# A transformer tower on one core: score groups turned in three blocks of 384 columns, and the end of the feed-forward written out

## The reference

```
h = keep the 179 best tokens of each batch (score x @ w, top k)
h = h + attention0(layernorm(h))   # 12 heads of 16
h = h + ffn0(layernorm(h))         # 192 -> 768 -> 192, weights, gelu and output rounded to a grid
h = h + attention1(layernorm(h))   # input rounded on ONE scale for all batches
h = h + experts(layernorm(h))      # 16 experts, each token goes to the best one

attention0: score[t, s] = sum_d tanh(q[t, d] + k[s, d]) * ws[d] + bs;  softmax over s;  @ v
attention1: xq = round(x / scale) * scale, scale = max|x| / 127 over all of x
            softmax with 2^floor(z) * (1 + frac z), z = logits / ln 2 - max
```

## Time and profile before

| what | value |
|---|---|
| device time, three runs | 1414.4 us median (1407.2 to 1414.99) |
| the profiled execution, its own time | 1418.28 us |
| its span, first to last instruction | 1416.4 us |
| PE busy | 1154.0 us (81%) |
| DVE busy | 1106.0 us (78%) |
| ACT busy | 1000.7 us (71%) |
| POOL busy | 862.3 us (61%) |
| mean granted clock of TensorE | 0.938 |

### The profile page before, as it was taken

How to read it: one execution, slowest core, us unless ns; L and a number is a source line. 1 busy time by engine, 2 the same in 40 slices (tenths; PEclk the granted TensorE clock), 3 DMA queues, 4 the chain that set the end, 5 groups by cost and what they waited for, 6 DMA issues and landing times. The chain is left out here.

```text
span 1416.4 us, 39002 instructions
## 1 busy us (share of the span) xinstructions
PE 1154.0 (81%) x16164; PEld 875.3 (62%) x16164; DVE 1106.0 (78%) x2109; ACT 1000.7 (71%) x921; POOL 862.3 (61%) x978
## 2 busy tenths in 40 slices
PE   4776888788878887887888779857999999998496
PEld 3454665566556655665556458844677777776496
DVE  8789999999999999999999958862556767675343
ACT  0479999999999999999999967732244334442142
POOL 4088888888888888889888976450012222123354
PEclk9899999999999999999999999975799999998598
DMA  9999998000000000000000011000000100001352
GB/s 251 360 359 359 355 341 294 4 2 3 2 2 2 2 2 2 2 3 2 2 2 2 2 33 37 0 1 1 1 2 10 54 17 18 18 17 32 98 157 62
DMA packets 75449, 103.06 MB, mean 73 GB/s; under 512 B 6303, under 2 KB 73640, under 8 KB 75282
## 3 DMA queue, kind: packets, MB, share of 16 engines
q1 hardware_dynamic: 63784, 87.90, 18.9%
q10 hardware_dynamic: 6860, 6.12, 1.7%
q0 software_dynamic: 4640, 6.65, 1.4%
HBM read 18.32 MB, written 83.85 MB: 72 GB/s over the span
## 5 line engine op out<-in xcount | busy, mean ns | idle before, releaser
L918 ACT ACTIVATE work<-work 128x2864 f32<-128x2864 f32 (+1 forms) x272 | 695.1, 2637 | 12.3 <-DVE work L437 11.4
L437 POOL TENSOR_TENSOR work<-shared 128x1253 f32<-128x1253 f32 (+1 forms) x272 | 613.7, 2266 | 130.5 <-PE psum L1786 94.2
L1786 PE MATMUL psum<-work,ws_place 128*32 128x179 f32 x8640 | 394.2, 321 | 150.2 <-ACT work L918 148.1
L437 DVE TENSOR_TENSOR work<-psum,shared 128x1611 f32<-128x1611 f32 (+3 forms) x288 | 487.9, 1722 | 0.6
L1786 PEld LDWEIGHTS psum<-work,ws_place 128*32 128x32 f32 x8640 | 257.0, 110 | 257.7 <-ACT work L918 205.5
L1975 PE MATMUL psum<-shared 32*64 32x179 f32 (+1 forms) x1728 | 140.3, 365 | 4.4 <-DVE peaks L1481 3.8
L1975 PEld LDWEIGHTS psum<-shared 32*64 32x64 f32 (+1 forms) x1728 | 80.6, 157 | 48.6 <-issue 35.4
L907 ACT ACTIVATE pt_region<-psum,bs_neg 128x512 f32<-128x512 f32 x144 | 104.3, 725 | 2.8 <-PE psum L1799 2.8
L805 POOL DMA_INDIRECT xs_dram<-w_store,slot_i x24 | 27.0, 1126 | 110.1 <-DVE slot_i L1588 90.7
L1276 DVE SCALAR_TENSOR_TENSOR p_sb<-psum,bs_col,s_top 128x358 f32<-128x358 f32 x144 | 82.2, 570 | 15.3 <-PE psum L1799 0.6
L1799 PE MATMUL psum<-ident,p_sb 128*128 128x128 f32 x544 | 91.6, 289 | 0.0
(11 more groups left out here) (365 smaller groups left out, 2002.2 us busy)
## 6 DMA issues: line engine op xcount, KB each, us to landing
xs_dram<-pad_row SPq DMA_DIRECT2D x23, 3088.0 KB, 27.6
pt_region<-xs_dram ACTq DMA_DIRECT2D x19, 193.0 KB
pt_region<-xs_dram SPq DMA_DIRECT2D x19, 193.0 KB, 2.4
xs_dram<-pad_row SPq DMA_DIRECT2D x1, 2895.0 KB, 27.1
work<-in_x SPq DMA_DIRECT2D x2, 768.0 KB, 10.2
work<-in_x ACTq DMA_DIRECT2D x2, 768.0 KB, 16.5
work<-in_L_ffn_W2T SPq DMA_DIRECT2D x1, 1536.0 KB
work<-in_L_ffn_W1T SPq DMA_DIRECT2D x1, 1536.0 KB
```

Of the source, the lines that this page charges most:

```text
L437: ins = eng.tensor_tensor(dst[:, a * KEEP:e * KEEP].rearrange("p (u s) -> p u s", s=KEEP), k[:, h * KP:h * KP + KEEP].unsqueeze(1).to_broa ...
L918: act.activation(a, a, ACT.Tanh).then_inc(tanh_done, 1)
L1786: ins = pe.matmul(bank_s[p % 2][32 * quad:32 * quad + 32, at:at + KEEP], ws_place[:, j, :], arg_slot(n)[:, u * KEEP:(u + 1) * KEEP], start ...
```

## The change

Five edits.

1. `p_sb` has a row of 192 (`ROW`) per group in place of 179, so that a full pair fills 384 columns: 128 + 64 keys of the first group, 128 + 64 of the second. `turn_duo` makes three blocks of it in place of four: block 0 holds keys 0 to 127 of the even group, block 1 keys 128 to 191 of the even group and 0 to 63 of the odd one, block 2 keys 64 to 191 of the odd one. `exps` takes 384 columns into three planes; the last pair of one group has two blocks as before.
2. In blocks 1 and 2 the keys stand on other partitions than in `v_sb`, so each batch needs V a second time in that order, `v_extra`. Three transfers on SP's queue copy it (64, 64 and 51 partitions), each batch after `v_ready`; the 24 fills of `xs_dram` are issued four to a batch after them, for the first six batches, in place of all at the start. `context` waits for the copy (`v_spread`).
3. `context` handles even and odd groups apart: rounds 0 and 1 are 16 products each of 96 columns, round 2 is 32 of 48 columns.
4. The end of the feed-forward is written out on DVE. Statistics come ahead of `norm_max`; the hidden layer of batch 15 is rounded before the output of batch 14 is added, and its product goes to `bank_pre`, so it doesn't wait for that addition. POOL normalises batches 12 and 13 itself; DVE computes mean and 1 / deviation of batches 14 and 15 (`last_pair`), which POOL's `pair_norms` then leaves out.
5. The maximum over partitions is a transpose on PE and a reduction on DVE in place of `partition_all_reduce`. `warm_up` has 8 products in place of 12 and waits for batch 13's maximum. Q, K and V of batch 0 have four banks (`qkv_bank`), and their waits go; `score_round(0, 1)` waits for what used to be waited for earlier.

The diff, cut to its core (counters of semaphores that only shift are left out):

```
+ROW, HALF_K, LAST_K = 192, 64, KEEP - 64
-        p_sb = [sb(f"p_sb{n}", [128, KEEP + WIDE]) for n in range(2)]
+        p_sb = [sb(f"p_sb{n}", [128, 2 * ROW]) for n in range(2)]
...
+        def qkv_bank(c, fill):
+            if isinstance(c, int) and c == 0:
+                return (bank_pre, bank_out, bank_s1, bank_pta)[fill]
+            return bank_out if fill else bank_pre
...
+            for b in range(B):
+                n, v = b % 2, v_sb[b % 2]
+                sp.wait_ge(v_ready, b + 1)
+                need(sp, v_spread[n], 48 * (b // 2))
+                sp.dma_start(v_extra[n][HALF_K:128, 0, :, :], v[0:HALF_K, 0, :, :]).then_inc(v_spread[n], 16)
+                sp.dma_start(v_extra[n][0:HALF_K, 1, :, :], v[HALF_K:128, 0, :, :]).then_inc(v_spread[n], 16)
+                sp.dma_start(v_extra[n][HALF_K:LAST_K, 1, :, :], v[0:TB, 1, :, :]).then_inc(v_spread[n], 16)
+                for k in range(4 * b, min(4 * b + 4, FILLS)):
+                    fill(k)
...
-            with pool.Fori(0, B // 2) as j:
+            with pool.Fori(0, B // 2 - 1) as j:
                 pair_norms(j, 0)
-            pool.wait_ge(x_maxed, 1)
-            pool.partition_all_reduce(x_allmax[:, :], x_max[:, :], 128, RMAX).then_inc(x_alled, 1)
+            for b in (B - 4, B - 3):
+                for t, rows in TILES:
+                    k = 2 * (b % 2) + t
+                    ins = pool.tensor_scalar(xn3[0:rows, 2 * b + t, :], resid[0:rows, b + 1, t, :], tmean[0:rows, k:k + 1],
+                                             trstd[0:rows, k:k + 1], ALU.subtract, ALU.mult)
+                ins.then_inc(norm_used, 1)
...
-                act.activation(pt[b % 2][:, :, 256 * k:256 * k + 128 * w],
-                               bank_pt[p % 2].rearrange("p (s c) -> p s c", s=2)[:, :, 0:128 * w],
+                act.activation(pt[b % 2][:, 0:w + 1, k, :],
+                               bank_pt[p % 2][:, 0:128 * (w + 1)].rearrange("p (s c) -> p s c", c=128),
                                ACT.Exp, bias=bs_neg[:, :], scale=1.0).then_inc(exp_done, 1)
...
-                    dve.tensor_scalar(p_sb[n][:, 2 * KEEP:KEEP + WIDE], p_sb[n][:, 2 * KEEP:KEEP + WIDE], bs_col[:, :], None, ALU.add)
+                    dve.tensor_scalar(p_sb[n][:, :], p_sb[n][:, :], bs_col[:, :], None, ALU.add)
...
-            staged(dve, ffn_step, (2, 5))
+            staged(dve, ffn_step, (2, 5), closed=True)
+            ffn_add(B - 4)
+            hidden_round(B - 3, 1)
+            dve.wait_ge(f_added, B - 3)
+            dve.wait_ge(stats_taken, B - 4)
+            pair_tile_stats(B - 3, 0)
+            norm_max(B - 7, 1)
+            ffn_add(B - 3)
+            hidden_round(B - 2, 0)
+            dve.wait_ge(f_added, B - 2)
+            pair_tile_stats(B - 2, 1)
+            norm_max(B - 6, 0)
+            hidden_round(B - 1, 1)
+            ffn_add(B - 2)
+            last_stats(0)
+            norm_max(B - 5, 1)
+            ffn_add(B - 1)
+            last_stats(1)
+            last_pair()
+            for b in range(B - 4, B):
+                norm_max(b, b % 2)
             dve.wait_ge(x_alled, 1)
+            dve.tensor_reduce(x_allmax[:, :], bank_k0[:, 0:128], AX.X, ALU.max).then_inc(x3_step, 1)
...
-                for a in range(duo(k)):
-                    for s in range(2):
-                        ins = pe.transpose(bank[:, 256 * s + 128 * a:256 * s + 128 * a + 128],
-                                           src[:, a * KEEP + 128 * s:a * KEEP + 128 * s + 128], ident[:, :])
+                for s in range(duo(k) + 1):
+                    ins = pe.transpose(bank[:, 128 * s:128 * s + 128], src[:, 128 * s:128 * s + 128], ident[:, :])
...
+                keys = [pt[n][:, s, :, :].rearrange("p k (i c) -> p k i c", c=32) for s in range(3)]
+                parts = [[(v_sb[n][:, 0, :, :], keys[0]), (v_sb[n][:, 1, :, :], keys[1])],
+                         [(v_extra[n][:, 0, :, :], keys[1]), (v_extra[n][:, 1, :, :], keys[2])]]
                 if r < 2:
+                    spans = [(KP * r, 16 * r, ((0, 6, 0), (0, 6, 16)))]
                 else:
+                    spans = [(100 * m, 16 * m, ((6, 9, 16), (5, 8, 0))) for m in range(2)]
...
             pe.wait_ge(f_added, B)
-            warm_up(12)
+            pe.wait_ge(n3_step, B - 2)
+            warm_up(8)
+            pe.wait_ge(x_maxed, 1)
+            pe.transpose(bank_k0[:, 0:128], x_max[:, 0:1].to_broadcast([128, 128]), ident[:, :]).then_inc(x_alled, 1)
```

More of the change, by code:

```diff
@@ L303, in build @@
         v_ready = sem("v_ready")
+        v_spread = [sem(f"v_spread{n}") for n in range(2)]
         args_dve = sem("args_dve")
@@ L322, in build @@
         wf_loaded = sem("wf_loaded")
-        w_step = sem("w_step")
         w_maxed = sem("w_maxed")
@@ L452, in staged @@
                     step(body * j + par, par)
-            for i in range(last, count + behind):
+            for i in range(last, last if closed else count + behind):
                 step(i, i % body)
@@ L575, in _ @@
             pool.memset(mx3[:, :], 0.0).then_inc(w1_step, 1)
+            for n in range(2):
+                pool.memset(v_extra[n][:, :, :, :], 0.0)
             pool.memset(pad_row[:, :], 0.0).then_inc(pad_ready, 1)
@@ L725, in _ @@
             pool.wait_ge(wq_step, 6)
-            pool.memset(stage[2][:, 1, 0:D], 0.0)
+            for n in (2, 3):
+                pool.memset(stage[n][:, 1, 0:D], 0.0)
             pool.memset(ew2[:, 1, :], 0.0).then_inc(ew_blank, 1)
@@ L1417, in norm_max @@
             def norm_max(b, par):
-                dve.wait_ge(pair_norm, b - par + 2)
+                last = isinstance(b, int) and b >= B - 2
+                means, rstds, first = (mean, rstd, 2) if last else (tmean, trstd, 0)
+                if isinstance(b, int) and B - 4 <= b < B - 2:
+                    dve.wait_ge(norm_used, b + 3)
+                    top_abs(b)
+                    return
+                if not last:
+                    dve.wait_ge(pair_norm, b - par + 2)
                 if isinstance(b, int) and b == 0:
@@ new lines, in last_pair @@
+            def last_pair():
+                cols = slice(2, 6)
+                mE, mO, vE, vO = (stats[:, cols, c] for c in (1, 4, 2, 5))
+                m, d, v, h, g, y, s = (a[:, cols] for a in (mean, diff, var, std, newt, rstd, above))
+                dve.tensor_tensor(m, mE, mO, ALU.add)
+                dve.tensor_tensor(d, mE, mO, ALU.subtract)
+                rlink(dve.tensor_tensor(v, vE, vO, ALU.add))
+                dve.tensor_scalar(m, m, 0.5, None, ALU.mult)
+                dve.tensor_scalar(v, v, 1.0 / D, EPS, ALU.mult, ALU.add)
+                rlink(dve.scalar_tensor_tensor(d, d, 0.25, d, ALU.mult, ALU.mult))
+                rlink(dve.tensor_tensor(v, v, d, ALU.add))
+                dve.tensor_scalar(h, v, -0.5, None, ALU.mult)
+                rlink(dve.tensor_copy(g, v.bitcast(I32)))
+                rlink(dve.tensor_scalar(g, g, -0.5, 1597463007.0, ALU.mult, ALU.add))
+                rlink(dve.tensor_copy(y.bitcast(I32), g))
+                for n in range(3):
+                    rlink(dve.tensor_tensor(s, y, y, ALU.mult))
+                    rlink(dve.tensor_tensor(s, s, h, ALU.mult))
+                    rlink(dve.scalar_tensor_tensor(y, s, 1.5, y, ALU.add, ALU.mult))
@@ L1806, in context @@
                 if r < 2:
-                    spans = [(0, UA // 4, 16 * r, col)]
+                    spans = [(KP * r, 16 * r, ((0, 6, 0), (0, 6, 16)))]
                 else:
-                    spans = [(UA // 4, PT_COLS // 32, 16 * n, col + UB * n) for n in range(2)]
-                for lo, hi, c, at in spans:
-                    for s, tile in ((0, first), (1, second)):
+                    spans = [(100 * m, 16 * m, ((6, 9, 16), (5, 8, 0))) for m in range(2)]
+                for at, c, groups in spans:
+                    for odd, (lo, hi, shift) in enumerate(groups):
@@ L1816, in context @@
+                            for step, (v, key) in enumerate(parts[odd]):
+                                ins = pe.matmul(cols, v[:, 4 * r + j, :], key[:, lo:hi, :, c + 4 * j:c + 4 * j + 4],
+                                                start=(step == 0), stop=(step == 1))
                 return ins
@@ L1952, in qk_mm @@
                     need(pe, ctx1_ready, c - 1)
-                if fill == 2:
+                if fill == 2 and c:
                     pe.wait_ge(qk_out, ROUNDS * c + 2)
                 x = xqT[c % 2]
-                bank = bank_out if fill else bank_pre
+                bank = qkv_bank(c, fill)
                 for col in range(2):
```

147 lines of the change are left out of this document (85 added, 62 removed).

## The result

| | before | after |
|---|---|---|
| median of 12 runs each | 1413.97 us | 1402.76 us |
| profiled execution | 1418.28 us | 1402.21 us |
| its span, mean granted clock | 1416.4 us, 0.938 | 1400.0 us, 0.942 |

A forecast was written before the change was run, and what follows sets the result against it. ACT, without idle time, bounds the first attention; a single-file chain at half clock bounds 930 to 998 us. Terms -12.8 + 0.6 + 0.3 - 3.8 - 2.4 - 2.7 - 1.5 = -22.3 us from median 1414.4 gave 1392, range 1380 to 1406.

The forecast's parts named there:

- The exponentials (-12.8): First attention: 128 exponentials go from 512 to 384 columns, 0.100 us each, -12.8 us, as nothing covers ACT.
- the one on `context` and the fills: First attention: doubled `context` products fit in PE's idle time, fills and V copies land in time: nothing for each.
- Rival B: First attention: DVE becomes the bound and all 12.8 us are lost, 1405; chance 0.13.
- Rival C: First attention: short `context` products cost over 25 ns each, POOL is late, ACT waits, 1440; chance 0.05.
- The end of the feed-forward (-3.8): Feed-forward end: the new order has POOL's chain as the later one, maximum at 951.6 instead of 955.38, -3.8 us.
- The maximum (-2.4): After the feed-forward: the maximum over partitions moves from POOL to PE, 4.26 us down to 1.8, -2.4 us.
- Q, K and V (-2.7): Batch 0, second attention: 40 products run without waits and the clock rises some 5.2 us in, 8.54 to 5.8, -2.7 us.
- the clock (-1.5): Second attention's first scores run at full clock for two to three rounds, -1.5 us; rest of batch 0 at half clock.
- part 2: Feed-forward end through batch 0's first scores: terms of 3.8, 2.4, 2.7 and 1.5, together 10.4 us.
- Rival A: Second attention: the clock stays up for all of batch 0, 6 to 8 us more gain, 1385; chance 0.17.
- D: Batch 0: clock does not rise in the dense run, -2.1 instead of -2.7, nothing for scores, 1394; 0.65 including the forecast.
- The start (+0.3): Kernel start: DVE adds the bias to 384 columns of two buffers in place of 77, +0.3 us.

The follow-up runs named there:

- e12: e6 repeated in more rounds: 1384.53 us, ratio 0.9786.
- e7: The changed kernel, fills in place, with the context's second round moved from group 5 to group 6: 1407.54 us, ratio 0.9965.
- e3: The kernel before with only the new feed-forward end, the maximum by TensorE and four banks for batch 0's products: ratio 0.9924.
- e9: e6 with the maximum over partitions taken by GpSimd again: 1389.22 us, timed once.
- e10: e6 with batch 0's Q, K and V products in two banks again: 1401.98 us, timed once.
- e5: The kernel before with its 23 fills moved as in e1: ratio 1.0015.
- e1: The changed kernel with fills moved: four at batch 0, then two a batch behind the context rounds: 1391.14 us, ratio 0.9877.
- e6: The changed kernel with four fills a batch, those of batches 1 to 5 behind the context rounds: 1387.56 us, ratio 0.9816.

## Why the prediction was wrong

**The exponentials (-12.8): right as a term, wrong in the sum.** 0.11 us each, and 12.4 to 13.5 us off the stage in each of the seven kernels in which fills and doubled context don't meet (732.93 to 734.04 against 746.44). As built the stage gave 2.2. Of the 11.3 us between after and e12 9.7 are ACT's waits; 1.4 are ACT's own busy time in the stage (733.09 and 731.71 us), for which no cause is shown.

**The failed step** is the one on `context` and the fills, costed apart and each at nothing. In its place the runs show PE without instructions where the two meet, ACT 9.7 us without sums, and all but 2.2 of the 12.8 us lost. The rule I set, that ACT waits only if PE is late by over 3 us in one place, was right in kind and too mild: the stalls of the four pairs, 2.5 to 4.6 us each in sum, cost ACT 1.1 to 4.6. I bounded the delay by the records' own duration (0.5 and 0.8 us), and that bound held: 64 records of 96 columns take 475.05 to 476.40, 1.35 us where I had allowed 1.7. I gave the fills "nothing" for their bytes. What I did not ask is what else uses the DMA engines while they are full: PE's own instructions. The page of the kernel before had the row of q8 (127 packets, 2.08 MB), and the GB/s slices showed full engines to 250 us; the two together, with the number of records that the change puts in one place, should have raised the question, though no row of before has the 7 us that a block takes. Rival B, whose time I gave as 1405, came nearest in number and is wrong in cause: DVE is at 95% and loses nothing from 500 us on. Rival C had the right shape (PE late, POOL late, ACT waits) and the wrong cause and size.

**The end of the feed-forward (-3.8).** 130.79 to 125.92, -4.9. Two other kernels with the old end have 128.93 and 129.08, so it is worth 3 to 5 us. (e7, which has the new end, has 129.89; its cause is open.) The +0.6 for the longer `context` at the head of this stage did not come: it is 125.92 with it and 125.93 without it, in e3. POOL's chain is the later one, as forecast; DVE in time, after:

```profile
944.03 0.55 DVE L1476 TENSOR_REDUCE mx<-work 128x2 f32<-128x384 f32 x1 [1.19 <-POOL work L812]
945.94 0.55 DVE L1476 TENSOR_REDUCE mx<-work 128x2 f32<-128x384 f32 x1 [1.35 <-POOL work L812]
...
948.91 0.19 DVE L1546 TENSOR_REDUCE x_max<-mx 128x1 f32<-128x32 f32 x1
...
950.46 0.29 DVE L1548 TENSOR_REDUCE x_allmax<-psum 128x1 f32<-128x128 f32 x1 [1.36 <-PE psum L2205]
950.78 0.15 DVE L1550 TENSOR_SCALAR x_scale<-x_allmax 128x1 f32<-128x1 f32 x1
```

**The maximum (-2.4).** 4.26 to 1.87, as said, but e9 shows that against GpSimd in the new order it is 1.5, and 0.65 at the scores: there the products start later, and the first 30 take 4.08 us where they take 4.68 in e12.

**Q, K and V (-2.7) and the clock (-1.5).** 8.54 to 5.59, -2.95, and from the first scores to the later row shown under e10 11.70 to 8.78, -2.9: the clock's term was too small against this execution of the kernel before. Against e5, where the clock rose in the old code too (7.03, then 8.13 us), the two are worth -1.4 and +0.65. That part 2 in all came to 10.7 us for my 10.4 is in part luck. The clock by stretches, after:

```profile
955.00:960.00 5.00, 5.00 (x41) 4.71 (x39) 0.29 (x1) 2.67 (x6) 0.00 (x0) 0.61 0.01 3
960.00:965.00 5.00, 3.59 (x54) 2.08 (x48) 4.42 (x6) 0.00 (x0) 0.00 (x0) 1.00 0.00 0
965.00:970.00 5.00, 4.05 (x30) 3.24 (x31) 1.18 (x5) 0.66 (x2) 0.00 (x0) 0.57 0.00 0
970.00:990.00 20.00, 19.02 (x141) 12.02 (x139) 7.00 (x13) 5.87 (x9) 0.00 (x0) 0.50 0.00 1
```

It rises at the end of the 40 products, as I let it, the first scores run at 1.00, and by 970 us it is 0.50 again. Rival A did not come, D neither. In e10, with two banks, the first 54 matmul records of the scores take 7.00 us as before (3.98 in e5 and after the change). The start (+0.3) was +0.6, from 78.15 to 78.79, but that start moves from 76.69 to 80.56 us over the runs.

Had the fills been put behind the context, the forecast of 1392 would have stood, as near as this can be told: it is 0.984 of 1414.4, and e1, e6 and e12 have 0.9877, 0.9816 and 0.9786.

## What to carry to other kernels

A transfer that saturates the DMA engines isn't free for an engine that uses none of its bytes, as here the instructions come over the same engines in blocks (q8). Where a change adds many short records, look at the row of the instruction queue, count the products between block ends, and compare the time that the engine needs for one block with the time that it takes to arrive under the transfer; then put big background writes where the instruction stream is thin. Two edits that are each free can cost together: sum what they do to a shared resource at the moment when they meet.

## What the runs showed of the hardware

- A block of 254 to 255 PE records (127 matmul records and their loads) came 6.95 to 7.21 us after the last, stall end to stall end, while fills ran at about 360 GB/s; its own transfer took 0.92 us. Stalls of up to 3.66 us carry the mark "issue" in the profile.
- The longest stall also cost the clock: PE's granted clock was 0.59 in 296 to 300 us, and the four pairs of matmul records behind that stall lie 0.60 us apart, in place of 0.31 in the same place of another batch.
- Short products are cheaper than I had bounded: 64 matmul records of 48 columns start within 1.00 us (480.72 to 481.72, after the change), 15.6 ns each. The Trainium skill, "TensorE: Matmul & The Clock Gate", section "Wait — 56ns, not 53.3ns?", has about 25 ns as a floor between starts; for these 32-row outputs, four beside each other, the measurement decides, and there is no such floor.
- The second attention and what follows took 431.0 to 447.6 us without a difference in its code behind batch 0's Q, K and V, 440.72 and 433.85 in two executions of one kernel (mean granted clock over the span 0.939 and 0.949). That is more than most terms of this sum, and a reason to compare stages and not spans.
